# Tensor product stage of a graph network: three products of the inputs, the gate and the edge rows on GpSimd, around its gather

## The reference

```python
r = edge_vec / jnp.linalg.norm(edge_vec, axis=1, keepdims=True)
s1 = jnp.concatenate([xs[:, :8], xd[:, :8]], axis=1)                      # source and destination
v1 = jnp.concatenate([xs[:, 8:].reshape(E, 8, 3), xd[:, 8:].reshape(E, 8, 3)], axis=1)
w = _mlp(emb, fc1_w1, fc1_w2)                                             # four 16 x 8 matrices an edge
vdot1 = jnp.einsum('euk,ek->eu', v1, sh1) / SQRT3
s_t = a1 * (s1 . Wss + vdot1 . Wvv)
v_t = a1 * ((s1 . Wsv) * sh1 + v1 . Wvs)
w2 = _mlp(emb, fc2_w1, fc2_w2)                                            # six 8 x 8 matrices an edge
scal, gates, vecs = ...                                                   # the same once more, from s_t and v_t
edge_out = jnp.concatenate([jnp.tanh(scal), (vecs * jnp.tanh(gates)[:, :, None]).reshape(E, 24)], axis=1)
edge_out = edge_out * norm[:, None]
return jax.ops.segment_sum(edge_out, edge_dst, num_segments=num_nodes)
```

## Time and profile before

| | |
|---|---|
| Median of 3 runs | 31319.55 us (31306.85 to 31346.87) |
| The profiled execution, its own time | 31347.26 us |
| Its span | 31345.4 us |
| Busy over the span | PE 25548.6, PEld 16798.5, DVE 18784.1, ACT 4500.2, POOL 16699.4 us |
| Indirect gathers of this stage (L2027) | 3125 |
| Mean granted TensorE clock of the execution | 0.669 |

### The profile page before, as it was taken

One profiled execution on the slowest core, in us unless ns is written; L12 is line 12 of the kernel. 1 busy time (PEld: TensorE's weight loads), 2 busy tenths in 40 slices (PEclk: granted clock), 3 DMA queues, 4 the chain that ended last, 5 costly groups with the idle time before them and its releaser, 6 DMA issues. The chain is left out here.

```text
span 31345.4 us, 606960 instructions
## 1 busy us (share of the span) xinstructions
PE 25548.6 (82%) x149627; PEld 16798.5 (54%) x149628; DVE 18784.1 (60%) x47074; ACT 4500.2 (14%) x12240; POOL 16699.4 (53%) x16857
## 2 busy tenths in 40 slices
PE   8777776666678888858999986675888888888888
PEld 6444442222248888826777766664444444444444
DVE  9211115666653333325666668997777777777777
ACT  4111111111110000011111111221111111111111
POOL 0677777777767777716777763332333333333332
PEclk9555555555555555556665565656999999999999
DMA  2111112222221111113333355443332333333222
GB/s 65 34 30 30 30 30 50 51 51 50 51 38 25 25 25 25 25 14 74 79 79 77 80 71 107 124 124 81 70 71 70 71 70 71 71 71 72 71 70 64
DMA packets 2615644, 1869.03 MB, mean 60 GB/s; under 512 B 1600556, under 2 KB 2081066, under 8 KB 2613815
## 3 DMA queue, kind: packets, MB, share of 16 engines
q1 hardware_dynamic: 1914438, 1424.41, 18.6%
q0 software_dynamic: 516000, 217.22, 6.8%
q10 hardware_dynamic: 184400, 220.54, 2.8%
HBM read 1621.01 MB, written 238.82 MB: 59 GB/s over the span
## 5 line engine op out<-in xcount | busy, mean ns | idle before, releaser
L2027 POOL DMA_INDIRECT rows_x<-x_table,index x3125 | 3022.1, 967 | 6780.0 <-DMA index<-in_src 6018.0
L1295 POOL DMA_INDIRECT rows<-x_table,index x3625 | 3445.4, 950 | 2025.7 <-issue 1254.1
L162 PE MATMUL banks<-rows,onehot 128*128 128x33 f32 (+1 forms) x14440 | 3417.0, 413 | 1058.5 <-issue 586.6
L547 POOL DMA_INDIRECT rows<-x_table,index x3125 | 3021.7, 967 | 1853.5 <-DMA index<-in_src 927.2
L162 PEld LDWEIGHTS banks<-rows,onehot 128*128 128x128 f32 x14440 | 3186.1, 328 | 1366.1 <-issue 1357.0
L905 POOL DMA_INDIRECT bucket_pairs<-pair,place_int x3125 | 3150.0, 1008 | 1275.6 <-issue 1213.5
L696 POOL DMA_INDIRECT rows<-x_table,index x3125 | 3142.5, 1006 | 1019.6 <-issue 952.0
L1891 PE MATMUL banks<-first,same_unit 128*128 128x384 f32 (+1 forms) x10000 | 3503.3, 476 | 0.0
L1205 DVE CUSTOM_DVE_ANT_0 junk<-banks,mask 128x320 f32<-128x320 f32 x5800 | 2551.1, 486 | 1563.1 <-PE banks L1240 1540.7
L1760 DVE TENSOR_TENSOR second<-banks,h 128x384 f32<-128x384 f32 (+1 forms) x5000 | 2309.6, 485 | 1068.7 <-PE banks L1891 1015.0
L1879 PE MATMUL banks<-u_turned,w_tensor 32*128 32x384 f32 (+1 forms) x10000 | 2119.5, 501 | 530.9 <-DVE first L1752 530.7
(11 more groups left out here) (395 smaller groups left out, 39498.7 us busy)
## 6 DMA issues: line engine op xcount, KB each, us to landing
key_row<-key_rows SPq DMA_DIRECT2D x1450, 320.0 KB
h<-hidden_dram SPq DMA_DIRECT2D x10000, 40.0 KB
key_row<-dst_rows SPq DMA_DIRECT2D x625, 320.0 KB, 3.4
rows<-x_table,index POOLq DMA_INDIRECT x9875
a_dram<-a ACTq DMA_DIRECT2D x625, 160.0 KB
a<-a_dram SPq DMA_DIRECT2D x625, 160.0 KB
rows_dram<-rows ACTq DMA_DIRECT2D x725, 90.0 KB
x_rows<-rows_dram SPq DMA_DIRECT2D x725, 90.0 KB
```

The costliest lines, as they stand in the source:

```text
L162: mm = nc.tensor.matmul(m["ps"][7][:, 0:width], m["onehot"][j % 3][:, t * P:(t + 1) * P], rows[:, t, :], start=t == 0, stop=t == T - 1)
L547: nc.gpsimd.indirect_dma_start(out=m["rows"][j][:, t * W:t * W + F], out_offset=None, in_=m["x_table"], in_offset=bass.IndirectOffsetOnAxi ...
L1295: nc.gpsimd.indirect_dma_start(out=m["rows"][j][:, t * XA:t * XA + F], out_offset=None, in_=m["x_table"], in_offset=bass.IndirectOffsetOnA ...
L2027: nc.gpsimd.indirect_dma_start(out=m["rows_x"][j][:, t * F:(t + 1) * F], out_offset=None, in_=m["x_table"], in_offset=bass.IndirectOffsetO ...
```

## The change

POOL's stream becomes a turn like those of the other engines: the two products and the sum of the front for group g+1 (`pool_front`), the gather for group g+4 (`pool_gather`), then the weighting and the gating of group g-2 (`pool_rows`). DVE keeps only the join of the front (L1737, now L1736) and loses `dve_bound` and `dve_rows`. POOL makes the sum over three axes by two additions, in place in `dots`, with a new semaphore `paired`. ACT's tanh waits until POOL has used the last `bounded` (`gated`), DVE's totals until POOL has used the last `vectors` (`edge_rows`), and DVE's memset behind `rows_owned` for the slot before. PE's and SP's streams are as before. The diff, without the list of semaphores, to which `paired` is added:

```diff
@@ -1711,6 +1711,7 @@
 
     def act_tanh(act, i, j):
         act.wait_ge(s["summed_up"], ONE + SLOTS * i + j + 1)
+        act.wait_ge(s["gated"], ONE + SLOTS * i + j)
         nc.scalar.activation(m["bounded"][:, :], m["unbounded"][:, :], ACT.Tanh).then_inc(s["bounded"], 1)
 
     def act_turn(act, i, j):
@@ -1730,17 +1731,54 @@
     def dve_front(dve, i, j):
 
         g = SLOTS * i + j
-        u, r = blocks(), axes(g)
-        part = m["dots"][:, :].rearrange("p (t c w) -> p t c w", t=T, c=3)
         dve.wait_ge(s["copied"][j], ONE + i + 1)
         dve.wait_ge(s["owned"], ONE + g + 1)
         nc.vector.tensor_reduce(m["u"][:, :].rearrange("p (b w) -> p b w", w=F)[:, :, K16 + U8:F],
                                 m["ps"][0][:, 0:T * OWN].rearrange("p (b k w) -> p b w k", k=PIECES, w=U8), AX.X, ALU.add).then_inc(s["joined"], 1)
-        dve.wait_ge(s["joined"], ONE + g + 1)
-        nc.vector.tensor_tensor(part, u[:, :, 0:3, K16:2 * K16], rep(r, 3, K16), ALU.mult).then_inc(s["multiplied"], 1)
-        nc.vector.tensor_tensor(u[:, :, 0:3, 0:K16], rep(u[:, :, 3, K16:2 * K16], 2, 3), rep(r, 3, K16), ALU.mult)
-        dve.wait_ge(s["multiplied"], ONE + g + 1)
-        nc.vector.tensor_reduce(u[:, :, 3, 0:K16], part.rearrange("p t c w -> p t w c"), AX.X, ALU.add).then_inc(s["prepared"], 1)
+
+    def pool_front(pool, i, j):
+
+        g = SLOTS * i + j
+        u, r = blocks(), axes(g)
+        part = m["dots"][:, :].rearrange("p (t c w) -> p t c w", t=T, c=3)
+        pool.wait_ge(s["joined"], ONE + g + 1)
+        nc.gpsimd.tensor_tensor(part, u[:, :, 0:3, K16:2 * K16], rep(r, 3, K16), ALU.mult).then_inc(s["multiplied"], 1)
+        nc.gpsimd.tensor_tensor(u[:, :, 0:3, 0:K16], rep(u[:, :, 3, K16:2 * K16], 2, 3), rep(r, 3, K16), ALU.mult)
+        pool.wait_ge(s["multiplied"], ONE + g + 1)
+        nc.gpsimd.tensor_tensor(part[:, :, 0, :], part[:, :, 0, :], part[:, :, 1, :], ALU.add).then_inc(s["paired"], 1)
+        pool.wait_ge(s["paired"], ONE + g + 1)
+        nc.gpsimd.tensor_tensor(u[:, :, 3, 0:K16], part[:, :, 0, :], part[:, :, 2, :], ALU.add).then_inc(s["prepared"], 1)
+
+    def pool_gather(pool, i, j):
+        pool.wait_ge(s["indexed"][j], 16 * (i + 1))
+        pool.wait_ge(s["copied"][j], ONE + i)
+        pool.sem_inc(s["going_pool"], 1)
+        for t in range(T):
+            nc.gpsimd.indirect_dma_start(
+                out=m["rows_x"][j][:, t * F:(t + 1) * F], out_offset=None, in_=m["x_table"],
+                in_offset=bass.IndirectOffsetOnAxis(ap=m["index"][j][:, t:t + 1], axis=0),
+            ).then_inc(s["gathered"][j], 16)
+
+    def pool_rows(pool, i, j):
+
+        g = SLOTS * i + j
+        rows = cut(m["rows"][j][:, :], t=T)
+        pool.wait_ge(s["bounded"], ONE + g + 1)
+        nc.gpsimd.tensor_tensor(rows[:, :, 0:K16], cut(m["bounded"][:, :], t=T), rep(m["strength"][:, bass.ds(g * T, T)], 2, K16),
+                                ALU.mult).then_inc(s["gated"], 1)
+        pool.wait_ge(s["vectored"], ONE + g + 1)
+        pool.wait_ge(s["gated"], ONE + g + 1)
+        nc.gpsimd.tensor_tensor(rows[:, :, K16:ST].rearrange("p t (w c) -> p t c w", c=3),
+                                m["vectors"][:, :].rearrange("p (t c w) -> p t c w", t=T, c=3),
+                                rep(rows[:, :, 0:U8], 2, 3), ALU.mult).then_inc(s["edge_rows"], 1)
+
+    def pool_turn(pool, i, j):
+        if there(i, j, 1):
+            pool_front(pool, *at(i, j, 1))
+        if there(i, j, 4):
+            pool_gather(pool, *at(i, j, 4))
+        if there(i, j, -2):
+            pool_rows(pool, *at(i, j, -2))
 
     def dve_first(dve, i, j, q):
 
@@ -1769,6 +1807,7 @@
         summed = cut(m["summed"][:, :], t=T)
         dve.wait_ge(s["returned"], ONE + g + 1)
         nc.vector.tensor_tensor(along, out[:, :, 1:4, 0:K16], rep(r, 3, K16), ALU.mult).then_inc(s["along"], 1)
+        dve.wait_ge(s["edge_rows"], ONE + g)
         nc.vector.tensor_tensor(vectors, rep(out[:, :, 0, K16:K16 + U8], 2, 3), rep(r, 3, U8), ALU.mult).then_inc(s["vector_parts"], 1)
         dve.wait_ge(s["along"], ONE + g + 1)
         nc.vector.tensor_reduce(summed, along.rearrange("p t c w -> p t w c"), AX.X, ALU.add).then_inc(s["totalled"], 1)
@@ -1776,24 +1815,6 @@
         nc.vector.tensor_tensor(vectors, vectors, out[:, :, 1:4, K16:K16 + U8], ALU.add).then_inc(s["vectored"], 1)
         dve.wait_ge(s["totalled"], ONE + g + 1)
         nc.vector.tensor_tensor(cut(m["unbounded"][:, :], t=T), summed, out[:, :, 0, 0:K16], ALU.add).then_inc(s["summed_up"], 1)
-
-    def dve_bound(dve, i, j):
-
-        g = SLOTS * i + j
-        dve.wait_ge(s["bounded"], ONE + g + 1)
-        rows = cut(m["rows"][j][:, :], t=T)
-        nc.vector.tensor_tensor(rows[:, :, 0:K16], cut(m["bounded"][:, :], t=T), rep(m["strength"][:, bass.ds(g * T, T)], 2, K16),
-                                ALU.mult).then_inc(s["gated"], 1)
-
-    def dve_rows(dve, i, j):
-
-        g = SLOTS * i + j
-        rows = cut(m["rows"][j][:, :], t=T)
-        dve.wait_ge(s["vectored"], ONE + g + 1)
-        dve.wait_ge(s["gated"], ONE + g + 1)
-        nc.vector.tensor_tensor(rows[:, :, K16:ST].rearrange("p t (w c) -> p t c w", c=3),
-                                m["vectors"][:, :].rearrange("p (t c w) -> p t c w", t=T, c=3),
-                                rep(rows[:, :, 0:U8], 2, 3), ALU.mult).then_inc(s["edge_rows"], 1)
 
     def dve_turned(dve, i, j):
 
@@ -1812,6 +1833,10 @@
                                         ALU.is_equal).then_inc(s["more_turned"], 1)
             dve.wait_ge(s["more_owned"], ONE + further + visits - 1)
             dve.sem_inc(s["going_dve"], 1)
+        if j:
+            dve.wait_ge(s["rows_owned"][j - 1], ONE + i + 1)
+        else:
+            dve.wait_ge(s["rows_owned"][SLOTS - 1], ONE + i)
         nc.vector.memset(m["done"][:, :], 0.0).then_inc(s["rows_owned"][j], 1)
 
     def dve_visits(dve, i, j, first, n):
@@ -1853,12 +1878,8 @@
             dve_turned(dve, *at(i, j, 2))
         if there(i, j, 0):
             dve_second(dve, i, j, 0)
-        if there(i, j, -2):
-            dve_bound(dve, *at(i, j, -2))
         if there(i, j, -3):
             dve_visits(dve, *at(i, j, -3), first, n)
-        if there(i, j, -2):
-            dve_rows(dve, *at(i, j, -2))
         if there(i, j, 2):
             dve_turned_further(dve, *at(i, j, 2), n_ahead)
         if there(i, j, 0):
@@ -2018,16 +2039,18 @@
 
         @block.gpsimd
         def _(pool):
-            with pool.Fori(0, ITERS) as i:
+            for j in range(3):
+                pool_gather(pool, 0, j)
+            pool_turn(pool, -1, SLOTS - 1)
+            for j in range(SLOTS):
+                pool_turn(pool, 0, j)
+            with pool.Fori(1, ITERS - 1) as i:
                 for j in range(SLOTS):
-                    pool.wait_ge(s["indexed"][j], 16 * (i + 1))
-                    pool.wait_ge(s["copied"][j], ONE + i)
-                    pool.sem_inc(s["going_pool"], 1)
-                    for t in range(T):
-                        nc.gpsimd.indirect_dma_start(
-                            out=m["rows_x"][j][:, t * F:(t + 1) * F], out_offset=None, in_=m["x_table"],
-                            in_offset=bass.IndirectOffsetOnAxis(ap=m["index"][j][:, t:t + 1], axis=0),
-                        ).then_inc(s["gathered"][j], 16)
+                    pool_turn(pool, i, j)
+            for j in range(SLOTS):
+                pool_turn(pool, ITERS - 1, j)
+            for j in range(2):
+                pool_turn(pool, ITERS, j)
 
         @block.scalar
         def _(act):
```

More of the change, by code:

```diff
@@ L2276, in build @@
                 stage_tensor_product(nc, m, sems(
-                    "tp", "going_dve joined owned more_owned hot_turned more_turned step to_root rooted finished stored added_up going going_pool multiplied prepared turned flipped brackets weighted "
+                    "tp", "going_dve paired joined owned more_owned hot_turned more_turned step to_root rooted finished stored added_up going going_pool multiplied prepared turned flipped brackets weighted "
                     "spread doubled contracted outputs_out returned along vector_parts totalled vectored summed_up bounded gated edge_rows "
```

## The result

The changed kernel takes 32543.8 us (median of 4 runs, 32482.7 to 32571.0) where the kernel before took 31331.2 in the runs beside it: a ratio of 1.0385 (95% interval 1.0367 to 1.0403), slower by 1213 us. The forecast was 32800, inside a range of 31700 to 34200.

The account below looks back on a forecast made before the run. It took PE's pace plus a stretch shared with DVE to bound a turn; POOL's path 399, clock falls 960 and further-visit turns 118 made +1477 us on 31347.3, 32824, stated as 32800 against the runs, range 31700 to 34200.

Parts of the forecast that it names:

- The bound: Last stage, plain turn of 13.22 us: 8.71 us to PE's first visit, then 4.51 at PE's pace to the next join.
- a shared stretch of PE and DVE: The 8.71 us from the join's start to PE's first visit, where DVE makes PE wait once, 0.55 us.
- The new path: Join, POOL's front, gather, rows, then PE's visit: 9.63 us instead of 8.71, 0.92 more per plain turn, 399 us.
- The clock: TensorE's clock falls in 7 of 10 plain turns after PE's idle stretches, 3.16 us each, 960 us.
- two of 1.0 and 0.85: PE's idle stretches in us per plain turn, before the transposes and before the visit, expected to bring clock falls.
- The sum: Whole kernel: 399 + 960 + 118 = +1477 us, giving 32824 on the profiled execution, stated as 32800 against the runs.
- The others were to lose 118: Turns with a further visit lose the 0.62 us by which the transposes come later: 191 x 0.62 = 118 us.
- The clock did not hold: Rival 1, last stage: the clock holds and only 399 + 118 = +517 us is lost, about 31840; chance 0.25.
- GpSimd was not twice as slow: Rival 2: POOL's operations take twice DVE's time, path 11.13 us, clock falls in every plain turn, about 34040; chance 0.20.
- The quick POOL: Rival 3: front and rows stay under 1.57 us, PE's visit waits for nothing, -334 us, about 30990; chance 0.04.
- The signs named ahead: Changed profile: visit released by POOL some 9.6 us after the join, POOL unpaused, PE waiting for `u`, clock about 0.8.
- PE should wait about 1 us for u: Sign at PE's transposes, which wait for POOL's front: start at 2.56 instead of 1.94 us, PE idle 1.0 us before.

Follow-up runs that it names:

- rows_only: Changed kernel with only gate and edge rows on POOL, behind the gather, and the front back on DVE; 31318.2 us, 0.9977 of the kernel before.
- rows_first: Changed kernel with POOL's turn in the order front, rows, gather, nothing else different; 31677.4 us, 1.0088 of the kernel before.
- front_only: Changed kernel with only the front on POOL, ahead of the gather, and gate and edge rows back on DVE; 31423 us, 37 us above the kernel before.
- gathers3: Changed kernel with three of a turn's five gathers ahead of the rows, two behind, on a slower chip; 36657 us, 1.002 of the kernel before beside it.
- changed_again: The changed kernel run once more, unaltered, on another slower chip; 38140 us, 1.042 of the kernel before beside it.

## Why the prediction was right, step by step

- **The bound.** "a shared stretch of PE and DVE" of 8.71 and 4.51 from the visit's start: held. Removing 1.78 us from DVE won nothing in a plain turn. In rows_only, without the front's delay, plain turns are at 13.23 as before.
- **The new path.** That POOL's front, gather and rows would close a loop through PE's visit is what the waits for L1771 and rows_first show. Its size was forecast as 9.63; it is 10.73 in the turn above and 10.44 in the median of all turns. In the mean of the plain turns the term is +1.64 us (8.91 to 10.55) and not +0.92. By parts, in that turn: join to POOL 0.18 (0.08 foreseen); front 1.89 (1.75); pause and gather 6.43 (6.33); rows and the step to them 1.52 (0.74), of which 0.58 is the overlap with L1663; to PE 0.06 (0.08). POOL's operations take 0.59 (240 elements), 0.35 (80) and 0.44 (120 undisturbed), where the line through the earlier trace rows gave 0.54, 0.25 and 0.32. By an estimate from 0.352 at 80 and 0.593 at 240, the fixed part is about 0.23 us, not the memset's 0.107, with 1.5 ns an element. The rule of the Trainium skill (GPSIMD Engine Reference, Performance versus the Vector engine) that GpSimd takes twice as long holds less here: 593 against 411 ns is 1.4 times, 352 against 230 1.5 times.
- **The clock.** That it would fall in 7 of 10 plain turns was right, by a choice that the prediction itself called one: it fell in 185 of 258 (slots 2 to 4). The term, 0.7 x 3.16 = 2.21 us, was too large: the mean from visit to join grew by 0.99 us (4.72 to 5.71). What failed is the price of a fall, 6.03 - 4.51 = 1.52 us and not 3.16. In the earlier trace rows, from which the 3.16 was taken, the visit itself was slow (2.34 us); in the turn above it still takes 1.30, and the slow rows begin behind it, so less of the stretch is at the low clock. And the cause was half wrong: of "two of 1.0 and 0.85" the first hurts little by itself (front_only, 13.40). The falls came only with the wait before the visit; whether that wait alone would bring them was not run.
- **The sum.** Plain turns: +2.67 us x 431 = 1151, foreseen 3.13 x 434 = 1359. Two errors of opposite sign met here, which was luck: of the parts of a turn, the chain took some 431 x 1.64 = 707 us where 399 were foreseen, the clock some 431 x 0.99 = 427 where 960 were. The others were to lose 118: the turns with a visit for the destination rows lost nothing (17.78 against 17.86), those for the sums 1.13 x 96 = 108. With -67 ahead of the stage this is the measured difference between the profiled executions, 1185 us.
- **The rivals.** The clock did not hold. GpSimd was not twice as slow. The quick POOL would have needed under 1.57 us for front and rows; they take 3.4 in the turn above.
- **The signs named ahead** came: visit released by POOL, no pause from front to gather to rows, clock below 0.92 (0.85; 0.8 was said). "PE should wait about 1 us for u" did not come in turns that start at the low clock: there the transposes are held up by PE itself.

## What to carry to other kernels

An engine that issues long gathers is idle by share and busy by order: work put behind the gather inherits its whole duration, and if the gather was started by what that work feeds, the two close a loop that nothing saved elsewhere can shorten. Before moving work to it, write down the distance from the event that starts its turn to the first consumer, and put what is waited for ahead of what is not; here one swap of two calls was worth some 920 us. A short wait on PE can cost more than itself: behind one of 0.9 us the clock fell in seven of ten turns here, for another 1.5 us each.

## What the runs showed of the hardware that was not expected

- A GpSimd product of 120 elements took 0.44 us alone and 1.01 us while DVE ran its one-hot operation with two SBUF inputs. The Trainium skill names this contention (GPSIMD Engine Reference, Key points: DVE instructions with two SBUF inputs); the trace agrees and gives its size.
- A start of POOL's work took 0.18 us from the join's end, where the earlier trace rows has 0.08 from ACT.
- On the slower chips the turns with a visit for the destination rows were 4.7 us longer in the changed kernel and not in gathers3, beside the wait of `second` in the plain turns. The wait before DVE's second one-hot matrix, by the views of waits over the whole span (total us, times, longest) of the changed kernel on the first chip, of changed_again, and of gathers3:

```profile
DVE hot_turned L1832 <- PE banks L1972: 163.6, 94, 2.3
```

```profile
DVE hot_turned L1832 <- DMA vectors_four<-vectors: 453.0, 87, 5.6
```

```profile
DVE hot_turned L1835 <- PE banks L1975: 231.9, 97, 3.4
```

The median wait before it is 1.9, 5.5 and 2.7 us. It follows a branch into the further visit; the releaser in the second row is a tile of another stage and so no cause. Why both waits depend on where POOL's gathers stand was not tried and stays open.
